# Four-layer graph network on one core: set-up loads and gathers in another order, zero fills moved into the softmax steps, and the gate biases added in one pass per pack

## What is computed

```python
edge_index = jnp.stack([src, dst])
x = _layernorm(x + _L0_gnn_ref(x, edge_attr_16, W_msg, b_msg, W_attn, b_attn, src, dst))  # edge softmax
x = _layernorm(x + _L1_gnn_ref(x, edge_index, W_tp, weight, bias))                        # bilinear messages
x = _layernorm(x + _L2_gnn_ref(x, edge_index, ...))                                       # two GIN layers, log-softmax
x = _layernorm(x + _L3_gnn_ref(x, src, dst, edge_type_8, edge_emb, w_ih, w_hh, b_ih, b_hh))  # typed messages, GRU

# L0: per edge a 16x16 message and a 16x16 score, softmax over the edges of a destination
w_m = (efeat @ W_msg + b_msg).reshape(E, in_f, -1);  w_a = (efeat @ W_attn + b_attn).reshape(E, in_f, -1)
h_src = feat[src][:, :, None];  e1 = w_m * h_src;  e2 = w_a * h_src
seg_max = jax.ops.segment_max(e2, dst, num_segments=N)
ex = jnp.exp(e2 - seg_max[dst]);  denom = jax.ops.segment_sum(ex, dst, num_segments=N)
ft = jax.ops.segment_sum(e1 * (ex / denom[dst]), dst, num_segments=N);  return ft.sum(axis=1)

# L3, the GRU at its end
gi = m @ w_ih.T + b_ih;  gh = features @ w_hh.T + b_hh
i_r, i_z, i_n = jnp.split(gi, 3, axis=-1);  h_r, h_z, h_n = jnp.split(gh, 3, axis=-1)
r = jax.nn.sigmoid(i_r + h_r);  z = jax.nn.sigmoid(i_z + h_z);  n = jnp.tanh(i_n + r * h_n)
return (1.0 - z) * n + z * features
```

## Time and profile before

| | us |
|---|---|
| three timed runs | 5056.15, 5062.51, 5062.52; median 5062.51 |
| profiled execution, its own time | 5059.33 |
| its span, first to last instruction | 5057.5 |
| busy in the span: DVE, PE, POOL, ACT | 3545.8, 3257.9, 3176.8, 1651.4 |
| set-up, until the first L1391 of DVE | 72.0 |
| GRU stage, from the first L1228 of PE | 290.6 |

### The profile page before, as it was taken

The page is one execution under the profiler, slowest core; times in us unless marked ns, Lnnn a source line. Parts: engine busy times, 40 slices in busy tenths (PEclk is TensorE's granted clock), DMA queues, the critical chain, the costliest instruction groups (busy, mean ns, idle before and its releaser), DMA issues. The chain is left out here.

```text
span 5057.5 us, 56133 instructions
## 1 busy us (share of the span) xinstructions
PE 3257.9 (64%) x12357; PEld 2409.9 (48%) x12357; DVE 3545.8 (70%) x6121; ACT 1651.4 (33%) x4258; POOL 3176.8 (63%) x2763
## 2 busy tenths in 40 slices
PE   4999999999834444436998334453445537777685
PEld 2444444444424444435887334443344327777532
DVE  5999999999976555535888455644556765555688
ACT  2565565665522111103444111130111232222144
POOL 3677777777646888887888777707776017776000
PEclk9999999999986555558999665685666655655798
DMA  3111111111133334332221100040000220000022
GB/s 95 46 44 40 46 44 40 46 43 41 30 109 78 60 59 62 56 42 44 53 58 48 17 7 7 6 110 7 7 7 6 83 70 7 7 7 7 8 75 56
DMA packets 373579, 211.64 MB, mean 42 GB/s; under 512 B 105770, under 2 KB 343662, under 8 KB 373442
## 3 DMA queue, kind: packets, MB, share of 16 engines
q1 hardware_dynamic: 254162, 190.55, 13.2%
q0 software_dynamic: 119296, 19.68, 6.6%
HBM read 151.70 MB, written 58.34 MB: 42 GB/s over the span
## 5 line engine op out<-in xcount | busy, mean ns | idle before, releaser
L695 POOL DMA_INDIRECT extra<-x_t,srci x784 | 767.5, 979 | 505.7 <-issue 492.8
L1153 PE MATMUL ps<-arena 128*128 128x128 f32 x2976 | 659.7, 411 | 641.9 <-DVE arena L1612 590.0
L1153 PEld LDWEIGHTS ps<-arena 128*128 128x128 f32 x2976 | 613.8, 314 | 677.6 <-issue 670.3
L1058 PE MATMUL ps<-edge_in,wl 17*128 17x512 f32 x784 | 702.0, 1072 | 14.8 <-DVE arena L1403 12.6
L682 POOL DMA_INDIRECT sums<-cmb,sidx x392 | 610.7, 1558 | 136.4 <-issue 117.6
L644 POOL DMA_INDIRECT xg<-in_x,xidx x392 | 466.1, 1189 | 253.7 <-DVE xp L1379 134.6
L631 POOL DMA_INDIRECT ft_t<-fts,fidx x392 | 507.5, 1295 | 144.1 <-issue 118.2
L1612 DVE TENSOR_TENSOR arena<-jmask,ps 128x1024 f32<-128x1024 f32 (+1 forms) x186 | 227.0, 1220 | 499.9 <-ACT ps L897 492.8
L1629 DVE TENSOR_TENSOR arena<-arena,ps 128x128 f32 x1488 | 426.1, 286 | 182.7 <-DVE arena L1629 24.9
L695 POOL DMA_INDIRECT extra<-h_t,srci x392 | 370.7, 946 | 243.6 <-issue 243.6
L1096 PE MATMUL ps<-arena 128*128 128x128 f32 x992 | 224.6, 418 | 442.5 <-DVE arena L1480 345.6
(11 more groups left out here) (202 smaller groups left out, 5992.8 us busy)
## 6 DMA issues: line engine op xcount, KB each, us to landing
edge_in<-far_row SPq DMA_DIRECT2D x98, 256.0 KB
ain<-in_src_row SPq DMA_DIRECT2D x56, 448.0 KB, 3.7
sums<-zero SPq DMA_DIRECT2D x132, 144.0 KB, 3.0
arena<-rel_t SPq DMA_DIRECT2D x63, 256.0 KB, 4.1
x_t<-yout SPq DMA_DIRECT2D x28, 448.0 KB, 3.3
xin<-x_t SPq DMA_DIRECT2D x28, 448.0 KB, 4.4
extra<-x_t,srci POOLq DMA_INDIRECT x784, 2.3
ain<-x_t SPq DMA_DIRECT2D x28, 448.0 KB, 4.8
```

The source lines that it names most:

```text
L695: pool.indirect_dma_start(dy[:, t, :], None, table, bass.IndirectOffsetOnAxis(ap=srci[:, t:t + 1], axis=0)).then_inc(d_gathered[n % QUEUE] ...
L1058: last = pe.matmul(ps[k][:, h * ET:(h + 1) * ET], wl[:, (k * CH + h) * P:(k * CH + h + 1) * P], eft[b][:, :], start=True, stop=True)
L1153: last = pe.matmul(slot_sums(k, n)[:, j * P:(j + 1) * P], oneh[b][:, j * P:(j + 1) * P], placed[b][:, j * P:(j + 1) * P], start=True, stop ...
```

## The change

It has two parts that do not touch each other.

**Set-up.** SP loads the keys and `vrow` right after `srci`, and also `dst_t` and `next_t`, which get tiles of their own (`kdst`, `knext`); the constants follow. The 14 zero fills leave the set-up: three of them go behind the loads of each of the steps 0 to 3, and two behind those of step 4. POOL's wait for them stands now ahead of the first scatter. POOL gathers the features of the first two tiles first, then the rows. PE makes the `W_tp` product first, then the transpose of the slot table, the transposes of the first features, and then those of the slot rows (`turn_slots`). DVE's list is put in a new order: `far` and the slot table first, the constants' casts later, the split of the first tiles before the weights, and the slot rows last. The second pair of matmuls of step 0 waits for the copies of the slot tables.

**Gate biases.** The four gate tiles of a set now lie at equal distances in one tensor, so that one instruction of 512 columns adds all four biases of a pack.

```diff
-        prep = [extra[:, k * COLS:(k + 1) * COLS] for k in range(11)]
-        ka, kb, ko, kspare, vrow, vcnt = (prep[k].bitcast(I32) for k in range(6))
-        kt, kd, kt2, vsum, ones = prep[6:11]
+        prep = [extra[:, k * COLS:(k + 1) * COLS] for k in range(14)]
+        ka, kb, ko, kspare, vrow, vcnt, kdst, knext = (prep[k].bitcast(I32) for k in range(8))
+        kt, kd, kt2, vsum, ones, kend = prep[8:14]
...
-        gates = [[tile_of(k) for k in ks] for ks in ((3, 7, 8, 9), (1, 2, 4, 14))]
-        rh, nn, zx, mT = (tile_of(k) for k in range(10, 14))
+        gate_set = [extra[:, 0:4 * UNIT], arena[:, (N_ACC + 1) * UNIT:(N_ACC + 5) * UNIT]]
+        gates = [[t[:, a * UNIT:a * UNIT + W] for a in range(4)] for t in gate_set]
+        rh, nn, zx, mT = (tile_of(k) for k in (14, 11, 12, 13))
...
-            for t in range(NODE_TILES):
-                sp.dma_start(rows(ft_t, 0, t), tiled(zero[:, :])).then_inc(ft_zero, 16)
-
             wait(k_far, 1)
...
+                if static(i):
+                    for t in range(3 * c, min(3 * c + 3, NODE_TILES)):
+                        sp.dma_start(rows(ft_t, 0, t), tiled(zero[:, :])).then_inc(ft_zero, 16)
...
                 if inside(i, c - 5, TILES):
                     b = (c - 5) % 2
+                    if not later(i, c - 5, 1):
+                        pool.wait_ge(ft_zero, 16 * NODE_TILES)
...
             gather(0, 0)
+            row_gathers()
             gather(0, 2)
-            pool.wait_ge(ft_zero, 16 * NODE_TILES)
...
                         elif k == 0:
                             pe.wait_ge(w_made, TYPES)
+                        else:
+                            pe.wait_ge(slots_done, 3)
...
             transpose(0, 0)
+            turn_slots()
             softmax_steps(pe, step)
...
-                    for a in range(4):
-                        last = dve.tensor_tensor(gates[c % 2][a][:, g * P:(g + 1) * P].rearrange("p (j f) -> p j f", f=F),
-                                                 bank[:, a], bgate[:, a, :].unsqueeze(1).broadcast_to((P, PACK, F)),
-                                                 ALU.add)
-                    last.then_inc(u_g, 1)
+                    dve.tensor_tensor(gate_cols.rearrange("p a (j f) -> p a j f", f=F), bank,
+                                      bgate[:, :, :].unsqueeze(2).broadcast_to((P, 4, PACK, F)),
+                                      ALU.add).then_inc(u_g, 1)
```

More of the change, by code:

```diff
@@ L448, in _ @@
             sp.dma_start(srci[:, :], src_t).then_inc(src_in, 16)
+            sp.dma_start(ka, dst_row.rearrange("(p c) -> p c", p=P)).then_inc(keys_in, 16)
+            sp.dma_start(kb, prev_row.rearrange("(p c) -> p c", p=P)).then_inc(keys_in, 16)
+            sp.dma_start(vrow, first_row.rearrange("(a n) -> a n", a=1).broadcast_to((P, COLS))).then_inc(first_in, 16)
+            sp.dma_start(kdst, dst_t).then_inc(next_in, 16)
+            sp.dma_start(knext, next_t).then_inc(next_in, 16)
             sp.dma_start(cst[:, :], const).then_inc(cst_in, 16)
@@ L616, in _, with row_gathers @@
             pool.iota(sl_i[:, :], pattern=[[P, SQ]], base=0, channel_multiplier=1).then_inc(counted, 1)
[L618 to L622, removed]
+            def row_gathers():
+                pool.wait_ge(v_idx, 1)
+                for q in range(SQ):
+                    pool.indirect_dma_start(grow[:, q * P:(q + 1) * P].bitcast(I32), None,
+                                            dst_row.rearrange("(t e) -> t e", e=P),
+                                            bass.IndirectOffsetOnAxis(ap=sl_ti[:, q:q + 1], axis=0)
+                                            ).then_inc(v_rows, 16)
             def step(i, c):
@@ L1014, in _ @@
             pe.wait_ge(casts, 3)
[L1016 to L1024, removed]
             for u in range(F):
@@ L1250, in _, with split @@
         def _(dve):
+            def split(i, c):
+                if not inside(i, c, TILES):
+                    return
+                n = nth(i, c)
+                part = lambda a: xp[:, :, a, :]
+                dve.wait_ge(x_gathered, 32 * SUB * (n + 1))
+                if later(i, c, 1):
+                    dve.wait_ge(xT_ps, 2 * i + c)
+                dve.tensor_copy(part(0), xg[:, :, :]).then_inc(split_done, 1)
+                dve.wait_ge(split_done, 5 * n + 1)
+                dve.tensor_tensor(xr[0][:, :, :], xg[:, :, :], part(0), ALU.subtract).then_inc(split_done, 1)
+                dve.wait_ge(split_done, 5 * n + 2)
+                dve.tensor_copy(part(1), xr[0][:, :, :]).then_inc(split_done, 1)
+                dve.wait_ge(split_done, 5 * n + 3)
+                dve.tensor_tensor(xr[1][:, :, :], xr[0][:, :, :], part(1), ALU.subtract).then_inc(split_done, 1)
+                dve.wait_ge(split_done, 5 * n + 4)
+                dve.tensor_copy(part(2), xr[1][:, :, :]).then_inc(split_done, 1)
@@ L1299, in _ @@
             dve.tensor_scalar(sl_tab[:, 2 * SQ:3 * SQ], sl_gi[:, :], 1.0, None, ALU.add).then_inc(v_off, 1)
+            dve.wait_ge(next_in, 32)
+            dve.tensor_tensor(kend, kdst, knext, ALU.is_equal).then_inc(k_same, 1)
+            dve.tensor_tensor(kt2, kspare, kdst, ALU.subtract).then_inc(k_same, 1)
+            dve.wait_ge(k_same, 3)
+            dve.tensor_tensor(kt2, kt2, kend, ALU.mult).then_inc(k_m, 1)
+            dve.wait_ge(k_m, 1)
+            dve.tensor_tensor(ko, kt2, kdst, ALU.add).then_inc(k_idx, 1)
@@ L1300, in _ @@
+            dve.wait_ge(cst_in, 96)
+            dve.tensor_copy(io_8[:, :], node_of[:, 0:P]).then_inc(casts, 1)
+            dve.tensor_copy(repsel[:, :], repf).then_inc(casts, 1)
+            dve.tensor_copy(identb[:, :], ident).then_inc(casts, 1)
             dve.wait_ge(type_in, 16 * SQ)
             dve.tensor_copy(type_s[0:TILES, :], growt[0:TILES, :].bitcast(I32)).then_inc(v_cast, 1)
+            for b in range(2):
+                dve.memset(mx[b][:, :, :], FAR).then_inc(first_made, 1)
@@ L1302, in _ @@
+            split(0, 0)
             dve.wait_ge(v_turned, 1)
[L1303 to L1317, removed]
@@ L1358, in _ @@
                                   ALU.mult).then_inc(w_made, 1)
+            dve.wait_ge(v_b, 2)
+            dve.wait_ge(v_rows, 16 * SQ)
+            for q in range(SQ):
+                at = slice(q * P, (q + 1) * P)
+                dve.tensor_scalar(gint[:, at].bitcast(I32), grow[:, at].bitcast(I32), sl_base[:, q:q + 1], None,
+                                  ALU.subtract).then_inc(v_rel, 1)
+            dve.wait_ge(v_rel, SQ)
+            dve.tensor_scalar(gj.bitcast(I32), gint.bitcast(I32), PACK - 1, None, ALU.bitwise_and).then_inc(v_rel, 1)
```

83 lines of the change are left out of this document (32 added, 51 removed).

## The result

| | before | after |
|---|---|---|
| median of four runs, us | 5061.18 (5056.15 to 5062.52) | 5004.04 (4998.83 to 5011.85) |
| profiled execution, its span | 5059.33, 5057.5 | 4998.83, 4997.0 |

The ratio is 0.989 (95% interval 0.9873 to 0.9907): 57 us faster by the medians, 47 to 64 by the interval. The forecast was 5010, so the time agrees. I cut both executions at the places that the change touches, each time read from the rows of the first or the last instruction of a stage.

A forecast was written before the change was run, and what follows sets the result against it. DVE was taken to bound the softmax steps and GRU stage, a serial chain the set-up. Gains of 36.8 and 15 us, together 51.8, took 5059.33 to 5007.5; with 3.2 for the median 5010.7, said as 5010, range 5000 to 5026.

The forecast's parts named there:

- Constants: Set-up: with five tensors of 196 KB (0.98 MB, 3.7 us) ahead, the constants land at 13.7 us instead of 9.97.
- Meanwhile: Set-up, called free: slot indices ready at about 10 us, feature split done before 19, both early for what follows.
- Product, weights, slot rows: Set-up chain: PE's product takes 7.0 us, to 21.3; weights end at 27.8, slot rows at 30.3, their transposes at 32.9.
- First load: Set-up: the first tile's load is issued at 31.7 us, lands 2.5 us later at 34.2, and decides over PE's spreading.
- 36.8: Set-up's total gain in us: 33.9 from step 0 starting earlier, 2.9 more by step 1; bounds 30 and 40.5.
- The moved fills: Steps 0 to 4: cost nothing; if the cover failed, up to 4.5 us per group, 21 us for five groups.
- Gate biases: GRU stage: one bias pass takes 0.61 us per pack instead of 0.79; gain taken as 15 us, between 8.7 and 16.0.
- the falls to go: GRU stage: PE's wait shrinks to about 1.4 us, so its clock stops falling, worth 5.2 us over twelve intervals.
- A: Rival, GRU stage: the clock still falls, so the stage gains 8.7 us and the total is 5017; chance 0.22.
- B: Rival, set-up: crowded loads, or fills delaying loads or gathers, leave a gain of 25 to 30 us, some 5020; chance 0.15.
- C: Rival: POOL reaches its first scatter before the last fills, and most of 21 us comes back, 5028; chance 0.04.
- D: Rival, GRU stage: the pass over four gate tiles runs like a scan, 1.25 us per pack, total 5071; chance 0.02.

The follow-up runs named there:

- product_first: The fills_late kernel with the operand of the `W_tp` product loaded second under its own semaphore, PE not waiting for the other constants: 5002.6 us, ratio 0.9892.
- fills_late: The changed kernel with no zero fills in steps 0 and 1, and 5, 5 and 4 in steps 2, 3 and 4: 5011.68 us (one run).
- fills_head: The changed kernel with all 14 zero fills back in the set-up, behind the loads and ahead of the `far_row` store: 5009.91 us, ratio 0.9907.
- gru_delay: The changed kernel with one idle DVE addition of 896 columns ahead of the first bias pass of tiles 2 to 13: ratio 0.9935, GRU stage 299.3 us.

## Why the prediction was right

*Set-up, step by step.*

1. *Constants.* Landed at 15.3, not 13.7. The 0.98 MB ahead cost 5.3 us and not 3.7, more than either rate that I had worked out. That is 1.6 of the 3.0 us by which L1403 came late; product_first takes the product off this wait and the scores start 3.4 us sooner. POOL's gathers of features now run in the same time, from 4.43 on, and no run tells their part from that of the loads.
2. *Meanwhile.* The slot indices were ready at 11.7 instead of 10, since `vrow` landed at 7.9 only, and the split was done at 19.9, not before 19; neither held anything up, since PE was in the product from 16.0 to 23.0.
3. to 5. *Product, weights, slot rows.* The durations held: 6.98, 3.21 for the eight, and PE's first L1030 15.6 us behind the product's start, where the steps gave 16.0.
6. *First load.* Issued at 32.95, 1.25 late by what came before. It was the step that decides, as said. But it took 4.2 us to land, not 2.5: 1.7 us. I had taken the time of a plain load of 196 KB that came last in its row; this one spreads one row of DRAM over 128 partitions, and has others right behind it. Which of the two makes it slow stays open. In fills_late, fills_head (38.60 to 42.96) and product_first it took 4.75, 4.4 and 5.1.
7. *Scores.* 3.9 us (37.18 to 41.10), as said. L1403 at 41.1 and not 38.1.
8. *Step 1.* 10.0 us behind step 0, as said.

So **36.8** was 33.8, inside the bounds of 30 and 40.5 that the two unknown landings gave.

*The moved fills* cost nothing: POOL's first scatter does not wait for them, and DVE waits for no load in steps 1 to 4. With the fills out of the first two steps (fills_late) nothing was gained. How much of the set-up's gain hangs on their place the prediction didn't ask: 5.8 of 30.9 us, in the new order.

*Gate biases.* The pass takes 0.68, 0.60 from start to start, the interval is 17.4, the gain over the twelve intervals 224.8 - 208.8 = 16.0 us. That is 12 x 0.9 + 5.2, and the whole stage, with the first tiles, gained 16.2, where the prediction's own terms gave 16.4. The 15 that I took lay below them, and no term stood for the difference. The Trainium skill (VectorE: DVE Perf Modes, section "The TRN2 errata — SBUF-src ops pay a fixed extra latency per instruction") gives 691 ns for a float32 `tensor_tensor` of 512 columns, and the trace's 682 is 1% below; by its fixed part for each small instruction, 46 us would have been saved, and the trace shows 16, since small instructions in a row overlap.

*The clock.* I expected "the falls to go". The five costly ones went. Falls as such didn't: the sign that I had named, "granted clock 1.00 in nearly every interval", holds for seven of the twelve; four show 0.90, and the last, where PE runs out of work, 0.82. The step was right in what it counted and wrong in how it put it: what counts is where in the tile a fall begins. The Trainium skill (TensorE: Matmul & The Clock Gate, section "A second HAM failure mode: psum-queue depth-cycling") has short idles between groups of matmuls make the clock swing; in this kernel it still does, and the trace adds that a swing is free where the next reader of the banks is far off.

*The rivals.* A fell for this kernel, by what it said of the time; gru_delay shows its mechanism alive at a wait of 2.5 us. B was there in part: 3 us by constants and load, far less than its 7 to 12, and not by the fills. C and D fell. *The total:* 50 us by the profile's stages against 51.8, and 57 (47 to 64) measured. The 50 lie within that interval, and the difference within the 3356.6 to 3372.1 that the untouched stages vary by. Since totals vary by as much as that, the match of 5004 with 5010 says less than the stages do: there the set-up gave 3.0 us less than its sum and the GRU stage 1.2 us more than the 15.

## What to carry to other kernels

Before a stage where one engine is full, ask of each thing in the set-up whether its first consumer needs it, and write down the chain that is left: with loads and work in the new order, the bulk writes in front of it still cost 6 us of 31 here. Where the engine that waits for a bank drops its clock when the wait gets long, time saved on the engine that releases it counts for more than itself, 16 us for 11 here, and so does time added, 25 us for 12; so look at which wait a slow stretch follows and who reads next. Compare stages, not totals: untouched stages differed by more than 10 us between executions of one kernel.

## What the runs showed of the hardware that I had not expected

- A load of 256 KB that spreads one DRAM row over 128 partitions took 4.2 to 5.1 us from issue to the matmul that waits for it (four kernels), where 196 KB of plain rows took 2.5. It was as slow with no fills behind it, but in all four another load or fill was. In after, where loads were issued one behind the other, plain ones of 196 KB took 2.5 to 5.8 us, and `vrow`, a row spread in the same way, 5.7.
- TensorE at 1.2 GHz for a few us costs nothing where it begins behind the pause for ACT's copy (17.43 us, as at 2.4 GHz), and 1.0 to 1.7 us behind the pause for DVE's release.
- Costly falls became rarer by degrees as PE's wait for a bank shrank: behind 24 of 26 waits of 2.2 us and more, 3 of 19 from 1.75 to 2.0, none of 66 at 1.4 to 1.5, over thirteen traces. What decides between waits of one length, and on the four falls in eleven pauses of 1.8 to 1.9 us for ACT's copy, stays open.
